# Leaving out waits for counts that an engine has already passed

## The reference

```
x = x + 0.5 * ffn(layernorm(x));  x = x + attention(layernorm(x));  x = x + 0.5 * ffn(layernorm(x))
ffn(x):   xq, w = fp4(x), fp4(w)                    # blocks of 16 along the last dim, 8 grid values
          h = silu(xq @ gate.T) * (xq @ up.T)       # 256 -> 704
          return fp4(h) @ down.T                    # 704 -> 256
attention: q, k = rope(rmsnorm(q)), rope(rmsnorm(k))   # 16 heads of 16, v: 8 heads of 32
          a = softmax(causal(q k^T / 4));  a = a[even] - lambda * a[odd]
          return (layernorm(a @ v) * (1 - lambda_init)) @ Wproj.T
```

## Time and profile before

| | |
|---|---|
| median of 3 runs | 2110.51 us (2108.02 to 2113.64) |
| the profiled execution | 2114.67 us, of which the span of its instructions is 2112.9 us |
| instructions in the span | 39423 |
| busy: TensorE, ScalarE, VectorE, GpSimd | 1863.1, 1706.1, 1550.5, 1374.2 us |
| granted TensorE clock, mean | 0.983 of full speed |

### The profile page before, as it was taken

One profiled execution on the slowest core, in us unless ns is written; L12 is line 12 of the kernel. 1 busy time (PEld: TensorE's weight loads), 2 busy tenths in 40 slices (PEclk: granted clock), 3 DMA queues, 4 the chain that ended last, 5 costly groups with the idle time before them and its releaser, 6 DMA issues. The chain is left out here.

```text
span 2112.9 us, 39423 instructions
## 1 busy us (share of the span) xinstructions
PE 1863.1 (88%) x13634; PEld 784.6 (37%) x13634; DVE 1550.5 (73%) x3324; ACT 1706.1 (81%) x2531; POOL 1374.2 (65%) x1439
## 2 busy tenths in 40 slices
PE   2677999999998999999999898999999888999866
PEld 1243443343433434344432443444433333432223
DVE  7889988686747898777955988888866678741375
ACT  3455988979888898878989888888889889889952
POOL 8788886666645786677853876876854657640155
PEclk9899999999999999999999999999999999999998
DMA  4134454234222445243331445343341344220013
GB/s 127 31 67 81 84 85 75 58 68 79 43 48 45 74 75 103 56 78 59 73 64 21 80 78 91 69 83 54 58 93 32 58 81 81 60 49 1 11 34 72
DMA packets 477493, 136.16 MB, mean 64 GB/s; under 512 B 458224, under 2 KB 477040, under 8 KB 477296
## 3 DMA queue, kind: packets, MB, share of 16 engines
q1 hardware_dynamic: 477296, 133.65, 34.4%
HBM read 11.96 MB, written 8.39 MB: 10 GB/s over the span
## 5 line engine op out<-in xcount | busy, mean ns | idle before, releaser
L1061 ACT ACTIVATE probs<-psum 128x1024 f32<-128x1024 f32 (+3 forms) x1280 | 1069.5, 934 | 80.5 <-PE psum L1346 64.1
L1364 PE MATMUL psum_o<-probs,v_sb 128*32 128x512 f32 (+3 forms) x5120 | 569.3, 540 | 16.7 <-POOL probs L967 10.6
L1309 PE MATMUL psum<-w_gu_T,xT 128*128 128x512 f16 (+1 forms) x2304 | 504.5, 367 | 49.4 <-DVE hq L1143 14.3
L1346 PE MATMUL psum<-q_stack,k_stack 64*128 64x512 f16 (+3 forms) x2560 | 384.8, 352 | 81.8 <-ACT probs L1061 62.4
L1309 PEld LDWEIGHTS psum<-w_gu_T,xT 128*128 128x128 f16 x2304 | 213.7, 99 | 314.0 <-issue 48.2
L967 POOL TENSOR_SCALAR_AFFINE_SELECT probs<-probs 128x512 f32<-128x512 f32 x256 | 179.4, 707 | 204.7 <-ACT probs L1061 203.8
L1322 PE MATMUL psum<-w_down_T,hT 128*128 128x256 f16 x2176 | 265.9, 278 | 34.4 <-DMA hT<-h 21.4
L1346 PEld LDWEIGHTS psum<-q_stack,k_stack 64*128 64x128 f16 x2560 | 99.6, 93 | 494.7 <-ACT probs L1061 385.3
L934 POOL TENSOR_TENSOR hq<-grid,qscale 128x704 f32<-128x704 f32 x128 | 183.7, 1437 | 100.5 <-DVE grid L1160 100.5
L1322 PEld LDWEIGHTS psum<-w_down_T,hT 128*128 128x128 f16 x2176 | 209.6, 99 | 97.2 <-issue 30.3
L941 POOL TENSOR_TENSOR h<-hq,h 128x704 f16<-128x704 f32 x128 | 202.3, 1580 | 65.4 <-ACT h L1017 64.7
(11 more groups left out here) (120 smaller groups left out, 2355.1 us busy)
## 6 DMA issues: line engine op xcount, KB each, us to landing
xb<-L_attn_x SPq DMA_DIRECT2D x16, 512.0 KB, 4.1
out<-xb SPq DMA_DIRECT2D x16, 512.0 KB, 3.4
xT<-x SPq DMA_TRANSPOSE x128, 3.1
hT<-h SPq DMA_TRANSPOSE x128, 3.5
k_stack<-st SPq DMA_TRANSPOSE x64, 3.2
q_stack<-st SPq DMA_TRANSPOSE x64, 3.3
k_stack<-L_ffn_w_down SPq DMA_DIRECT2D x1, 704.0 KB, 4.1
k_stack<-L_ffn_w_gate SPq DMA_DIRECT2D x1, 512.0 KB, 5.3
```

Of the source, the lines that this page charges most:

```text
L1061: nc.scalar.activation(probs[:, s % 3, 2 * u:2 * u + 2, q0:CHUNK], psum[:, plan.pairs[s, u]:plan.pairs[s, u] + 2, q0:CHUNK], ACT.Exp, scal ...
L1309: last = nc.tensor.matmul(bank(e)[:, 0:hi - lo], xs[:, x, t % 2, k, :], w_gu_T[:, w, k, lo:hi], start=n == 0, stop=n == len(parts) - 1)
L1346: last = nc.tensor.matmul(psum[:, plan.pairs[s, u] + j, q0:CHUNK], k_stack[half, at, h, kt % NTC * P:(kt % NTC + 1) * P], q_stack[half, c ...
L1364: last = nc.tensor.matmul(psum_o[at:at + VD, q0:CHUNK], v_sb[:, kt // NTC % SLOTS * NTC + kt % NTC, 2 * g + u, :], probs[:, s % 3, 2 * u + ...
```

## The change

Each wait of the stage functions goes through a helper, `until`, which remembers for each engine and each semaphore the highest number waited for so far. A wait for a number no higher than that is not emitted. Stages, their order, buffers and the counts that they add are the same. The waits of the setup's own code (L1491 to L1775) are still written directly; the stages of the lead that run inside it go through the helper.

```diff
+        passed = {}
+
+        def until(engine, name, sem, n):
+
+            if passed.get((name, id(sem)), 0) < n:
+                engine.wait_ge(sem, n)
+                passed[name, id(sem)] = n
+
-        def wait_bank(engine, e):
+        def wait_bank(engine, name, e):
...
-                engine.wait_ge(exp_done, scored)
+                until(engine, name, exp_done, scored)
             for b, n in freed.items():
-                engine.wait_ge(bank_free[b], n)
+                until(engine, name, bank_free[b], n)
...
```

`wait_read` is changed in the same way, and every other `wait_ge` of the five stage functions becomes an `until` with the engine's name:

```diff
-                    sp.wait_ge(low_ready, LOW["low_" + kind, *e[1:]] + 1)
+                    until(sp, "sp", low_ready, LOW["low_" + kind, *e[1:]] + 1)
...
-                        act.wait_ge(low_ready, before)
+                        until(act, "act", low_ready, before)
...
-                    pe.wait_ge(*landed("x", pair))
+                    until(pe, "pe", *landed("x", pair))
```

More of the change, by code:

```diff
@@ L864, in sync_stages @@
                     c = e[1]
-                    wait_read(sp, [("down", 3, t) for t in range(NTC * c, NTC * (c + 1))])
+                    wait_read(sp, "sp", [("down", 3, t) for t in range(NTC * c, NTC * (c + 1))])
                     dst, src = rows(out_v, c)
@@ L997, in scalar_stages @@
                     if before:
-                        act.wait_ge(low_ready, before)
-                    act.wait_ge(rstd_ready, RSTD["rstd", pas, 2 * p // NTC] + 1)
+                        until(act, "act", low_ready, before)
+                    until(act, "act", rstd_ready, RSTD["rstd", pas, 2 * p // NTC] + 1)
                     for j in range(2):
@@ L1057, in scalar_stages @@
                     if s >= 3:
-                        act.wait_ge(values_done, s - 2)
-                    act.wait_ge(scores_full, 2 * s + u + 1)
+                        until(act, "act", values_done, s - 2)
+                    until(act, "act", scores_full, 2 * s + u + 1)
                     nc.scalar.activation(probs[:, s % 3, 2 * u:2 * u + 2, q0:CHUNK],
@@ L1120, in vector_stages @@
                     a, n, nb = buffers("x", pair)
-                    dve.wait_ge(early_normed, EARLY_NORM["norm_a", "x", *pair] + 1)
+                    until(dve, "dve", early_normed, EARLY_NORM["norm_a", "x", *pair] + 1)
                     block_scales(e, a, n, nb, -1e-12)
@@ L1134, in vector_stages @@
                     elif part == 1:
-                        dve.wait_ge(*full(h))
-                        dve.wait_ge(*read(("hidden", *e[1:3], 0)))
+                        until(dve, "dve", *full(h))
+                        until(dve, "dve", *read(("hidden", *e[1:3], 0)))
                         nc.vector.scalar_tensor_tensor(h2, h2, H_SCALE, bank(h)[:, 0:n], ALU.mult, ALU.mult)\
@@ L1146, in vector_stages @@
                     a, n, nb = buffers("h", e[2:])
-                    wait_read(dve, [("hidden", *e[2:], part) for part in range(len(PIECES))])
+                    wait_read(dve, "dve", [("hidden", *e[2:], part) for part in range(len(PIECES))])
                     block_scales(e, a, n, nb, neg_h_floor[:, 0:1])
@@ L1165, in vector_stages @@
                     down = ("down", pas, t)
-                    dve.wait_ge(*full(down))
+                    until(dve, "dve", *full(down))
                     nc.vector.scalar_tensor_tensor(xb[:, t % XB, :], bank(down)[:, 0:C],
@@ L1224, in vector_stages @@
                     s = [s for s in steps_of(steps, c) if steps[s][1] == g][-1]
[L1225 removed]
+                    until(dve, "dve", values_done, s + 1)
                     if COPIED_O[e]:
                         before = [k for k, v in COPIED_O.items() if v == COPIED_O[e] - 1][0]
[L1228 removed]
+                        until(dve, "dve", *full(("transpose_o", *before[1:])))
                     nc.vector.tensor_copy(o_sb[:, :], psum_o[:, :]).then_inc(o_copied, 1)
```

158 lines of the change are left out of this document (79 added, 79 removed).

## The result

The kernel after takes 2098.73 us (median of 6 runs, 2096.93 to 2104.13), the kernel before beside it 2111.62 (6 runs). The ratio is 0.9944, with an interval of 0.9929 to 0.9959: about 12 us faster.

What follows compares the result with a forecast made beforehand. No engine is full, so a path changing engines was taken to bound the kernel. Terms summed to 9.4 us; a third on the path, 3.1 us, off 2110.51 gave 2107.4, range 2101.0 to 2112.5.

Steps and rivals of the forecast that it cites:

- A satisfied wait costs nothing: Wait instructions whose count is there long before, mostly on TensorE running ahead of its array: price nothing.
- the rival at 2079.9: Each wait instruction costs its own time: TensorE's 599 at 51 ns, 30.6 us off; chance 0.03.
- My sign that a fall of over 6.3 us: Whole kernel: a fall of over 6.3 us would prove the forecast wrong, satisfied waits costing something after all.
- The sum of the places, 9.4 us: Stages where an engine stands on a wait that now rides: exps, scale stages, norm_a, TensorE, SyncE, 9.4 us together.
- Its largest term: VectorE's scale stages behind the gate: 28 times 0.16 us, 4.5 us, with a lower bound of 2.5 us.
- The share of one third: Part of the 9.4 us lying on the path, since about one of TensorE, ScalarE and VectorE carries it: 3.1 us.
- The step that failed: TensorE's removed waits cost only where it stands, a dozen places at 0.06 us: 0.7 us, between 0 and 1.9.
- The slower rival: SyncE issues transposes up to 0.05 us earlier, some overlap and land later: 10 us more, or 2120; chance 0.05.
- the instruction count: Sign in the profile after: about 37,385 instructions in the whole trace, from 39,423.
- the busy times: Sign in the profile after: busy times of all engines as before within 2 us.
- the scale stage's idle time behind the gate: Sign on VectorE: L1088's idle time behind L1143, 28 times and 5.6 us before, gone from the list.
- the median landing: Transposes' landing, 3.5 us median and 5.9 worst before; the slower case would need a median of about 3.9.

Runs made afterwards that it cites:

- the means over four phases: Four paddings of TensorE's program start each, without against with the rule on TensorE: 0.99835 against 0.99845 (other engines as before), 0.99608 with and 0.99583 without (rule on the others).
- rest184: Kernel before with the rule on ScalarE, VectorE, GpSimd and SyncE only, plus 184 wait instructions at TensorE's start; about 0.996 expected, its own measured ratio not in the text.
- the eight pairs: Kernels with the same TensorE program, with against without the rule on the four other engines: 0.0025 less in the mean, 5.2 us, between 3.6 and 7.0 each.
- The order experiment: Kernel after with last-coming waits written first so that they ride, at four paddings of TensorE's start: 0.9943, 0.9962, 0.9965, 0.9972; mean 0.99605 against 0.99608 unturned.
- pe_only: Kernel before with the rule on TensorE alone, 599 wait instructions fewer there, other engines as before: ratio 0.9969 to before.
- b32: Kernel before with 32 more wait instructions at the start of TensorE's program, no wait taken out: ratio 0.9963 to before.

## Why the prediction was wrong

- **A satisfied wait costs nothing** was right. At 51 ns each TensorE's 599 instructions would have given 30.6 us; no kernel here gained half of that, and the means over four phases differ by 0.0001 to 0.0003. So the rival at 2079.9 is excluded, as the pace of the matmuls said. A cost of a us or two in all is not excluded by the runs. My sign that a fall of over 6.3 us would mean that satisfied waits cost something was wrong too: the time can fall for another reason.
- **The sum of the places, 9.4 us**, was not measured by itself. Its largest term was too large: the traces show 0.09 to 0.10 us saved at a scale stage, not 0.16.
- **The share of one third** gave 3.1 us. The rule on the four other engines is worth 5.2 us in the runs. By what I wrote ahead of rest184 that is nearer to 6 us, waits that cost more than their places, than to 3. The replay puts 2.9 us of it on the waits and, over the eight pairs, about 2 us on landings, so by that estimate this term was near as a price of waits and low as the price of the removal. The order experiment warns that not even the 2.9 us is shown on the chip.
- **The step that failed** is the one that costed TensorE's removed waits at nothing but places where it stands (0.7 us): true for the instructions as far as four phases can tell, not for the kernel. I looked at what a removed instruction does where it stands and never asked what else its going moves. Taking out 599 shifts the later fetches against the transposes, and pe_only measured 0.9969 for that part alone, 6.5 us in place of 0.7. Padding with nothing removed does as much (b32, 7.8 us). I had the queues with instruction packets on the page of before and passed them over as 0.5% of the DMA engines' time.
- At the phases of before and after the ratio falls by 0.0031 with the rule on TensorE and by 0.0025 more with the rest, 6.5 and 5.3 us. That they add up to after is so by construction, and no test of the account. The kernel before sits at a bad phase (the worst of its four), after at the best of its four, and that is luck; it is why the change looks better than the 5 us or so that it is worth on average over the phases tried.
- **The slower rival** had the right object, the landings, and the wrong cause: by the runs above the time moved with other traffic beside the transposes. SyncE's earlier issue was not tested by itself.
- Of the signs I named, the instruction count (37,387 for 37,385), the busy times (within 2.7 us, a little over the 2 that I gave), the scale stage's idle time behind the gate (gone from the list) and the median landing (3.5 us, worst 5.3 against 5.9) came as said. The median hid the point: it is the tail that moved.

## What to carry to other kernels

When an edit changes the number of instructions in a long unrolled program, it also moves where that program's fetches meet the transfers on the path; price the edit over a few shifts of the fetches (padding in an idle stretch at the start) before believing a gain of half a percent. Four shifts still leave some 0.1% open here. Look at the tail of a landing, not its median, and at what else is on the DMA queues while it is slow. In this kernel a wait for a passed count showed no cost where the engine runs ahead; leaving waits out paid on the engines that stand.

## What the runs showed of the hardware

- A transpose lands 1.0 to 1.3 us later when a 16 KB fetch of TensorE's program starts 1.0 to 2.5 us after its issue (between 4.38 and 4.69 us in the mean, against 3.35); 92 to 100% of such landings are over 3.9 us. The 8 KB packets of q14 do so less: where one started 2.0 to 2.5 us after the issue and no q8 packet was near, 70 landings took 3.87 us in the mean, half of them over 3.9.
- As an estimate by replay, this is worth up to 11 or 13 us of 2110 here: cutting the landings to 3.5 us gains between 1.7 and 13.3 us in the 20 traces by the first replay, between 1.0 and 11.0 by the second.
- Runs of one kernel are longer at a lower granted TensorE clock: over 31 runs of before, with clocks of 0.975 to 0.984, it and the time correlate at -0.75, with 1.0 us per 0.001 of clock. In the four other rounds of before (18 to 27 runs) the correlation was between -0.38 and -0.80, so a part of the spread goes with it, and how large a part differs from round to round.
